# Lead products on TensorE, the last load's distances in halves, and masks made elsewhere in the order

## What is computed

```python
x = x + xattn(ctx_1024, layernorm(x))     # ctx_1024: (8, 64, 256), x: (8, 512, 256)
x = x + ffn(layernorm(x), w1, b1, w2, b2) # 256 -> 1024 -> 256, quantised to 8 bits
```

## Time and profile before

| what | value |
|---|---|
| median of 3 runs | 197.55 us (197.39 to 199.72) |
| profiled execution: time, span | 198.22 us, 196.4 us |
| busy share of the span | PE 52%, PEld 35%, DVE 78%, ACT 51%, POOL 10% |
| chain that ended last, by engine | DVE 57%, PE 23%, ACT 11%, issue 6%, DMA 2% |

### The profile page before, as it was taken

How to read it: one execution, slowest core, us unless ns; L and a number is a source line. 1 busy time by engine, 2 the same in 40 slices (tenths; PEclk the granted TensorE clock), 3 DMA queues, 4 the chain that set the end, 5 groups by cost and what they waited for, 6 DMA issues and landing times.

```text
span 196.4 us, 3730 instructions
## 1 busy us (share of the span) xinstructions
PE 103.0 (52%) x1240; PEld 68.5 (35%) x1251; DVE 152.8 (78%) x745; ACT 99.6 (51%) x173; POOL 20.6 (10%) x82
## 2 busy tenths in 40 slices
PE   0789941000450000000006648799999989997993
PEld 0778840000230000000002323465565656564672
DVE  1995757999999999999992696587878778786342
ACT  3784865299960000404400027867666665758740
POOL 8955452000000000000000000000000000000000
PEclk9999999555555555555555899999999999999999
DMA  5992004600000000011034210003030303021224
GB/s 179 348 349 91 7 5 184 246 0 2 3 0 2 0 0 0 0 68 67 0 107 72 39 24 3 0 0 110 0 107 0 110 2 107 19 92 36 71 80 138
DMA packets 15990, 13.10 MB, mean 67 GB/s; under 512 B 5857, under 2 KB 15586, under 8 KB 15842
## 3 DMA queue, kind: packets, MB, share of 16 engines
q1 hardware_dynamic: 14530, 12.56, 19.9%
q10 hardware_dynamic: 1440, 0.30, 0.7%
HBM read 7.35 MB, written 5.51 MB: 65 GB/s over the span
## 4 chain that ended last, share of the span: by engine, by line
DVE 57%; PE 23%; ACT 11%; issue 6%; DMA 2%; DVEq 0%; ACTq 0%
DVE Y L920 6%; DVE R L753 5%; PE y L1097 5%; ACT h_int L572 5%; DVE Dm L869 4%; DVE stats L852 4%; PE h L1083 4%; DVE X L847 4%; ACT M L566 3%; DVE A L721 3%; DVE enter L907 3%; DVE bcarry L906 3%; DVE carry L741 3%; DVE M L742 3%; PE t L1073 2%
## 5 line engine op out<-in xcount | busy, mean ns | idle before, releaser
L572 ACT ACTIVATE h_int<-h,b_s 128x512 int16<-128x512 f32 x64 | 43.1, 686 | 8.6 <-PE h L1083 7.7
L1097 PE MATMUL y<-w2T,XT 128*128 128x256 bf16 x256 | 37.7, 273 | 0.3 <-DVE XT L882 0.3
L1083 PE MATMUL h<-M,w1T 128*128 128x512 bf16 x119 | 36.0, 381 | 3.5 <-ACT h_int L572 1.7
L1110 PE MATMUL y<-w1T 128*128 128x512 bf16 x17 | 6.1, 515 | 47.8 <-DVE S_lo L934 47.8
L1097 PEld LDWEIGHTS y<-w2T,XT 128*128 128x128 bf16 x256 | 25.0, 98 | 12.4 <-DVE XT L882 0.5
L882 DVE TENSOR_SCALAR XT<-h_int 128x1024 bf16<-128x1024 int16 x32 | 13.1, 424 | 18.6 <-ACT h_int L572 18.4
L1110 PEld LDWEIGHTS y<-w1T 128*128 128x128 bf16 x19 | 2.1, 121 | 50.6 <-DVE S_lo L934 47.6
L578 ACT ACTIVATE code<-Y,shifts 128x640 bf16<-128x640 bf16 x3 | 2.5, 829 | 33.2 <-DVE enter L907 33.2
L1052 PE MATMUL t<-ident_bf,w_raw 128*128 128x128 bf16 x32 | 4.6, 311 | 21.8 <-ACT w_raw L536 20.6
L847 DVE TENSOR_TENSOR X<-e,X 128x512 f32<-128x512 f32 x16 | 10.2, 680 | 5.5 <-PE e L1063 5.5
L1083 PEld LDWEIGHTS h<-M,w1T 128*128 128x128 bf16 x128 | 10.4, 98 | 9.5 <-ACT h_int L572 4.9
(11 more groups left out here) (172 smaller groups left out, 232.1 us busy)
## 6 DMA issues: line engine op xcount, KB each, us to landing
X<-in_x_dram SPq DMA_DIRECT2D x8, 512.0 KB, 8.2
out_dram<-E SPq DMA_DIRECT2D x32, 128.0 KB, 1.8
w_raw<-in_L_ffn_w_dram SPq DMA_DIRECT2D x2, 1024.0 KB
S<-in_ctx_dram SPq DMA_DIRECT2D x1, 512.0 KB, 3.9
path_dram<-A SPq DMA_DIRECT2D x3, 160.0 KB, 1.8
path_dram<-XT SPq DMA_DIRECT2D x3, 160.0 KB, 1.9
R<-path_dram SPq DMA_DIRECT2D x24, 16.0 KB, 1.8
path_dram<-A SPq DMA_DIRECT2D x1, 128.0 KB, 1.9
```

Of the source, the lines that this page charges most:

```text
L572: nc.scalar.activation(h_int[:, g % 2, n, :], bank01[n % 2][:, :], ACT.Identity, bias=b1_s[:, n:n + 1], scale=1.0 / W_ONE).then_inc(h_roun ...
L1083: mm = nc.tensor.matmul(bank01[n % 2][:, :], w1T[:, k, n * P:n * P + P], xqT[:, g % 2, k, :], start=(k == 0), stop=(k == KH - 1))
L1097: mm = nc.tensor.matmul(bank67[t // 2][:, t % 2, :], hq[:, g % 2, n, t * P:t * P + P], w2T[:, n, :], start=False, stop=(n == NH - 1))
```

## The change

On PE, 40 products of 32 by 8 of the identity with itself go to bank5 as soon as the identity is made. `spread_rows(0)` goes ahead of `dots(0)`, `spread_rows(1)` ahead of `dots(1)`, `spread_rows(3)` ahead of `dots(2)`. The second half of `dots(3)` goes to bank `dist_banks[0]`, behind two waits, and each half signals on its own. DVE takes the moments of load 3 in two halves around `scales(0)`, its masks in two parts behind `scales(1)` and `scales(2)`, and the last distances in two halves with one add each. ACT does `spread(3)` ahead of `roots(1)`, and the roots of load 3 in halves. SP's wait ahead of the weights counts one signal more.

```diff
--- before.py
+++ after.py
@@ -29,6 +29,7 @@
 KH = D // P
 EPS = 1e-5
 LOADS = 4
+LEAD = 40
 CL = NC // LOADS
 UL = 2 * CL
 NG = NU // 4
@@ -312,7 +313,7 @@
             for k in range(LOADS):
                 for a in range(2):
                     load_x(sp, k, a)
-            sp.wait_ge(dot_done, LOADS)
+            sp.wait_ge(dot_done, LOADS + 1)
             sp.dma_start(w1_raw[:, :, :], w1.rearrange("(p n) d -> p n d", n=NH)).then_inc(w_loaded, 16)
             sp.dma_start(w2_raw[:, :, :], w2.rearrange("(n p) d -> p n d", p=P)).then_inc(w_loaded, 16)
             sp.dma_start(b2_raw[:, :], b2.rearrange("(o d) -> o d", o=1)).then_inc(w_loaded, 16)
@@ -443,20 +444,24 @@
 
         @block.scalar
         def _(act):
-            def roots(k):
-
-                halves = (norms[:, k, :, 0:HR], mirrored[:, k, :, :])
+            def roots(k, hs=None):
+
+                us = slice(0, UL) if hs is None else slice(CL * hs, CL * hs + CL)
+                made = 4 * k + 3 if hs is None else 4 * k + 3 * hs + 2
+                count = 2 * k + 2 * (hs or 0)
+                halves = (norms[:, k, us, 0:HR], mirrored[:, k, us, :])
                 for e in range(2):
-                    act.wait_ge(prods_made, 4 * k + 3 + e)
+                    act.wait_ge(prods_made, made + e)
                     nc.scalar.activation(halves[e], halves[e], ACT.Relu).then_inc(clamped, 1)
-                if k == 1:
-                    spread(LOADS - 1)
                 act.wait_ge(pool_const, 3)
                 for e in range(2):
-                    act.wait_ge(clamped, 2 * k + e + 1)
+                    act.wait_ge(clamped, count + e + 1)
                     n0 = CL * k if e == 0 else NC - CL - CL * k
-                    dst = bass.AP(E, 2 * CH * e + n0 * (TW + 1), [[SLOTS * EW, P], [CH, 2], [TW + 1, CL], [EW, HR]])
-                    nc.scalar.activation(dst, halves[e].rearrange("p (h c) i -> p h c i", h=2), ACT.Sqrt).then_inc(rooted, 1)
+                    at = 2 * CH * e + n0 * (TW + 1) + CH * (hs or 0)
+                    pairs = [[CH, 2]] if hs is None else []
+                    dst = bass.AP(E, at, [[SLOTS * EW, P], *pairs, [TW + 1, CL], [EW, HR]])
+                    src = halves[e].rearrange("p (h c) i -> p h c i", h=2) if hs is None else halves[e]
+                    nc.scalar.activation(dst, src, ACT.Sqrt).then_inc(rooted, 1)
 
             def spread(k):
                 act.wait_ge(spread_done, k + 1)
@@ -510,8 +515,11 @@
             for j in range(UL // 2):
                 copy_xT(3, j)
             spread(2)
-            for k in range(1, LOADS):
+            spread(3)
+            for k in range(1, LOADS - 1):
                 roots(k)
+            for hs in range(2):
+                roots(LOADS - 1, hs)
             act.wait_ge(ctx_rest, 1)
             nc.scalar.activation(S_mid[:, :, :], S_r1[:, :, :], ACT.Copy).then_inc(ctx_split, 1)
 
@@ -650,8 +658,11 @@
                                  (odd_batch[:, :], batch_of_u[:, :, :, :].rearrange("p q e c -> p (q e c)"))):
                     nc.vector.reduce_max(dst, src, mybir.AxisListType.X).then_inc(dve_order, 1)
                 nc.vector.tensor_scalar(order_low[:, :, :], order_raw[:, :, :], T - 1, None, ALU.bitwise_and).then_inc(dve_order, 1)
+                own[0] += 6
+
+            def more_masks():
+
                 v.wait_ge(pool_const, 14)
-                own[0] += 6
                 v.wait_ge(dve_order, own[0])
                 link(nc.vector.tensor_scalar(order[:, :, :], order_low[:, :, :], 1.0, None, ALU.add))
                 nc.vector.tensor_scalar(init0[:, :], first[:, :], -BIG, BIG, ALU.mult, ALU.add).then_inc(dve_order, 1)
@@ -690,6 +701,22 @@
                 nc.vector.stream_shuffle(mirrored[:, k, :, :].rearrange("p (h c) i -> p h c i", h=2),
                                          part[:, :, HR:I].rearrange("p (h c) i -> p h c i", h=2)[:, :, ::-1, :],
                                          mirror).then_inc(prods_made, 1)
+
+            def last_distances(hs):
+
+                k = LOADS - 1
+                v.wait_ge(dot_done, k + 1 + hs)
+                flat = dist_banks[k if hs == 0 else 0][:, :, :].rearrange("p a b -> p (a b)").rearrange("p (u i) -> p u i", i=I)
+                us = slice(CL * hs, CL * hs + CL)
+                at = UL * k + CL * hs
+                part = norms[:, k, us, :]
+                nc.vector.tensor_tensor(part, flat[:, us, :], rstd[:, at:at + CL].unsqueeze(2).to_broadcast([P, CL, I]),
+                                        ALU.mult).then_inc(prods_made, 1)
+                v.wait_ge(prods_made, 4 * k + 3 * hs + 1)
+                v.wait_ge(lengths_made, k + 1)
+                nc.vector.tensor_tensor(part, part, lengths[:, k % 2, us, :], ALU.add).then_inc(prods_made, 1)
+                v.wait_ge(prods_made, 4 * k + 3 * hs + 2)
+                nc.vector.stream_shuffle(mirrored[:, k, us, :], part[:, ::-1, HR:I], mirror).then_inc(prods_made, 1)
 
             def moments(k, j):
                 if j % (B // 2) == 0:
@@ -765,14 +792,22 @@
             load_moments(0)
             load_moments(1)
             load_moments(2)
+            for j in range(UL // 2):
+                moments(3, j)
             scales(0)
+            for j in range(UL // 2, UL):
+                moments(3, j)
             distances(0)
-            load_moments(3)
-            for k in range(1, LOADS):
-                scales(k)
-                distances(k)
+            scales(1)
             masks()
-            v.wait_ge(rooted, 2 * LOADS)
+            distances(1)
+            scales(2)
+            more_masks()
+            scales(3)
+            distances(2)
+            for hs in range(2):
+                last_distances(hs)
+            v.wait_ge(rooted, 2 * LOADS + 2)
             to_chunks(0, SLOTS // 4)
             v.wait_ge(skewed, 2)
             forward(0, 1)
@@ -959,6 +994,8 @@
         @block.tensor
         def _(pe):
             pe.wait_ge(ident_made, 2)
+            for i in range(LEAD):
+                nc.tensor.matmul(bank5[0:TW, 0:8], ident[:, 0:TW], ident[:, 0:8], start=True, stop=True)
 
             def ctx_T():
 
@@ -980,6 +1017,11 @@
                 flat = dist_banks[k][:, :, :].rearrange("p a b -> p (a b)")
                 pe.wait_ge(xT_copied, (UL // 2) * (k + 1))
                 for h in range(2):
+                    if h and k == LOADS - 1:
+                        mm.then_inc(dot_done, 1)
+                        pe.wait_ge(std_ready, LOADS)
+                        pe.wait_ge(sum_copied, LOADS)
+                        flat = dist_banks[0][:, :, :].rearrange("p a b -> p (a b)")
                     for a in range(CL):
                         at = (CL * h + a) * I
                         for kk in range(KH):
@@ -1020,19 +1062,19 @@
             turns(0)
             turns(1)
             pe.wait_ge(ctxT_copied, 4)
+            spread_rows(0)
             dots(0)
-            spread_rows(0)
             turns(2)
-            dots(1)
             pe.wait_ge(std_ready, 1)
             pe.wait_ge(sum_copied, 1)
             spread_rows(1)
+            dots(1)
             turns(3)
             pe.wait_ge(std_ready, 2)
             pe.wait_ge(sum_copied, 2)
             spread_rows(2)
+            spread_rows(3)
             dots(2)
-            spread_rows(3)
             pe.wait_ge(std_ready, 3)
             pe.wait_ge(sum_copied, 3)
             dots(3)
```

## The result

The changed kernel is faster, by half of what was forecast: a median of 196.49 us (195.61 to 198.94, 20 runs) against 197.96 us (20 runs of the kernel before), ratio 0.9926, 95% interval 0.9907 to 0.9944. That is 1.5 us; 3.0 were forecast. The profiled execution took 196.50 us with a span of 194.7. Medians are of all executions, and ratios are of the fast ones alone, since a few executions of any kernel here take about a per cent longer at a lower granted clock.

What follows compares the result with a forecast made beforehand. Bound: PE's code-paced products until 30.66 us, then DVE with the masks last, to the transposes at 35.30. Masks 1.3, PE's end 1.15 and halves 0.55 give −3.0 us: 194.5 us; range 193.1 to 196.7 with rivals 1 and 2.

Steps and rivals of the forecast that it cites:

- Pauses follow edges of 256 instructions: PE's pauses in the distance products come where its code blocks of 256 instructions end; four pauses, 3.99 us together.
- rival 3: PE's pauses belong to places in the work, not code blocks, so all four stay; 195.55 us, chance 0.06.
- The first pause: PE's pause in dots(0), until 18.71 us, goes because lead products make block 449 be asked for 5 us earlier.
- rivals 1 and 4: Loads hold PE's first new code block: passed at 18.7 us (196.6, chance 0.15) or 20.75 us (198.7, chance 0.04).
- rival 1: Loads hold PE's first new code block, edge 449 passed at 18.7 us as before; 196.6 us, chance 0.15.
- The masks hide: DVE's masks, 2.8 us ahead of the forward pass, run under waits instead; their place is worth 1.3 us.
- PE's wait for POOL's parts: PE waits ahead of dots(2) for POOL's parts of load 3, due at 23.45 us; dots(2) starts at 23.65.
- The halves on DVE: The last load's distances on DVE in two halves, 1.25 and 1.22 us; halves are worth 0.55 us in all.
- Rival 2: PE's last pause, in dots(3), goes too; dots(3) ends at 27.5 us, ACT becomes the bound; 193.7 us, chance 0.14.
- The pause that the forecast had at dots(1): PE pauses at code edge 705 in dots(1), 3.5 to 4.1 us after 15.2, taken as 19.1 us.
- the walk of DVE: DVE's new order: rstd(3) at 25.7, distances(2) until 27.6, lengths(3) at 27.4 us, all before PE's first half at 28.45.
- PE's end: PE finishes the last distance products at 29.4 us instead of 30.56, worth 1.15 us.

Runs made afterwards that it cites:

- e8: The changed kernel with 20 lead products instead of 40; median 198.44 us, ratio 0.9999 to the kernel before.
- e1: The changed kernel plus 12 products in PE's wait ahead of spread_rows(3), to keep the clock up; median 196.97 us, ratio 0.9944 to the kernel before.
- e3: The kernel before with the 40 lead products alone added; median 197.20 us, ratio 0.9958.
- e4: The kernel before with only the masks moved, in two parts behind scales(1) and scales(2); median 197.14 us, ratio 0.9956.
- e2: The changed kernel without the 40 lead products; median 195.47 us, ratio 0.9886 to the kernel before.
- e5: The changed kernel without lead products, POOL's lengths of load 2 held back until the fourth inverse; median 195.14 us, ratio 0.9859 to the kernel before.
- the pair on one chip: The changed kernel with and without lead products, both run again on the same chip; medians 196.65 and 195.78 us.
- e9: The changed kernel without lead products, the masks' second part moved ahead of the third inverse; median 195.50 us, ratio 0.9861 to the kernel before.

## Why the prediction was half right

**Right.** Pauses follow edges of 256 instructions: in e8 they stand at the recorded instructions 449, 705 and 1217, in e1 at 1217, wherever in the work these fall, and in the changed kernel and e3 the old places have none (rival 3 falls). The first pause went, since the block was asked for earlier; the loads did not hold it (rivals 1 and 4 fall: the packet started at 10.24, in their midst). The time measured, 196.49, is next to rival 1's 196.6, but that is chance: the pause until 18.7 that makes its sum is not there. The masks hide, worth 1.1 us alone (e4) where 1.3 were forecast. PE's wait for POOL's parts was named, with the right releaser. The halves on DVE took 1.11 and 1.21 us where 1.25 and 1.22 were forecast, ACT's end 1.0 for 1.18. Rival 2's sign was there, no pause in dots(3), but for a reason that it did not have: PE ran at half the clock, and with the clock kept up the pause came back (e1). The pause that the forecast had at dots(1) did not come either.

The Trainium skill ("Runtime: NRT & Kernel Launch", Instruction fetch mechanics) calls an edge's cost mostly hidden. The trace doesn't agree: one edge cost up to 2.88 us (e8).

**Wrong: the step that failed.** It is the walk of DVE: "Rstd(3) at 25.7, distances(2) 25.7 to 27.6, lengths(3) at 27.4, all before 28.45", by which DVE would wait for PE's first half. DVE came to the last load at 30.48 and not at 27.6, 2.9 us late, and by then PE's first half was long done. The 2.9 us have five parts:

- *The last load, 0.6 us, put at nothing.* The second half of the moments of load 3 was to run from 16.63. The load isn't complete before 17.2, in the kernel before either (which came to it only at 19.34). So even without lead products the third inverse comes at 24.04 and not at 23.45 (e2).
- *The fetch among the loads, 0.64 us, put at nothing.* "Block 449 is asked for 5 us earlier": I asked whether the loads would hold the fetch, not what the fetch would do to the loads. One 16 KB packet made a part of later loads 1.5 us late. DVE's moments of load 2 waited for it 1.1 us, and load 3's first half was complete at 16.41 instead of 15.17, so that the first inverse came at 17.76 and not 16.45, and the third at 24.68 where e2 has 24.04.
- *The masks' second part, 0.85 us, mis-sized.* It was put at 1.9 us and took 2.8 (24.91 to 27.68), since it ran beside POOL's lengths(2). With that out of the way it took 1.9 (e5). "The other masks run beside dots(2), the last edge's pause giving the room" was the sentence: there was no room, DVE itself was the bound.
- *Dots(2) at half the clock, 0.42 us, put at nothing.* The forecast has 1.9 us for dots(2) behind a wait of PE; it took 3.12, and DVE stood still for it.
- *The additions of `distances(2)`, 0.4 us*, beside POOL's lengths(3).

DVE had 1.0 us to spare in the forecast (27.6 to 28.58), which leaves 1.9 us; less 0.4 that the halves and ACT were quicker, this is the 1.5 us between 32.3 and 33.80. The last two parts stand for each other: with the clock kept up the wait is gone and the additions take as much more (e1). Of the three gains forecast (masks 1.3, PE's end 1.15, halves 0.55) PE's end is the one that is missing: it moved from 30.56 to 30.40 only, since POOL's parts came at 24.82 for 23.45 and the last two blocks of code stand behind them; the clock made no difference to that end (e1).

**So where the expected gain went.** In the order of the kernel before the lead products bring PE's end 2.0 us forward (e3); in the changed order, nothing (30.40 with them, 30.26 without). And PE was not alone in front: with the masks at the end DVE and POOL stood 1 us behind it, and in the changed order DVE was busy without a break. The lead products' price, late loads, fell on the engine that had become the bound: without them the start is 0.65 us earlier (e2), and 0.9 in the pair on one chip, although pauses of PE's code are back.

## What to carry to other kernels

A dummy instruction is not free because its engine idles: count how far it moves the edges at which an engine fetches code, look at when those fetches start, and ask what shares the DMA engines with them at that moment. Before valuing a pause on the critical engine, remove it on paper and see which engine is next and how far behind; here it was one microsecond. Work moved "into a wait" needs the wait of the other engines looked at too: what runs on POOL beside it can make it longer.

## What the runs showed of the hardware

- **One instruction fetch went with a late part, one in 16, of every load behind it.** 1.15 us of packet, and the last part of the fifth load 1.4 to 1.5 us behind the other 15, in five profiles out of five with that fetch at 10.2 to 10.5 us. That fetch started 0.9 to 1.1 us after its edge was passed (9.1 to 9.6 us). In the eight other profiles the same edge was passed at 14.0 to 14.9 us, also while the loads ran, and the fetch started 1.4 to 2.3 us after it (15.9 to 16.3). Why these differ is open.
- **DVE beside POOL.** An addition of nine elements out of SBUF took 0.95 us while POOL added 128x512 f32, 0.16 otherwise; it ended with POOL's (e2, e5). The same happened to other instructions with both operands in SBUF: `order_back` in e4 (1.00 us), an addition of 128x256 in e9 (1.27 us, 0.42 otherwise).
- **Tiny f32 products at the start cost 55 ns each** (80 in 4.44 us, 40 in 2.30; the forecast had at most 2.5 for 80). Which clock they had is not shown: the profile gives 1.00 for these first microseconds, yet the same eight 128x128 transposes of the context, from 8.7 or 8.8 us on, took 1.91 us in the changed kernel and 1.24 in e1.
- **When the clock rises behind the way back differs from execution to execution.** PE idles there for 45 us and more and starts at half the clock (1.2 GHz). It rose to full (2.4 GHz) 2.8 us after the first weight load in e2, 4.4 in the changed kernel, 5.5 in e3, and from that weight load to the end the span took 90.8, 91.8 and 92.4 us; the ten other profiles lie in between: a microsecond later in the rise, some 0.6 us more in the end. The windows of the first 5 us, of e2 and then of the changed kernel, show it (the granted clock stands behind the engines' busy times: 0.72 and 0.56):

```profile
102.24:107.24 5.00, 4.05 (x21) 1.74 (x22) 0.50 (x1) 0.00 (x0) 0.00 (x0) 0.72 0.40 59
```

```profile
102.89:107.89 5.00, 4.99 (x22) 1.81 (x22) 0.00 (x0) 0.00 (x0) 0.00 (x0) 0.56 0.40 59
```

This is 1.0 of the 1.7 us by which the single profiles of e2 and the changed kernel differ in span; the other 0.65 is the start.
